# The last 17 slot tiles of the second feed-forward pass in two column halves, and the first chunk's rows in a buffer of their own

## The reference

```
x = x + 0.5 * ffn(layernorm(x))     # 8 experts, top 2, hidden width 352
x = x + attn(layernorm(x))          # 6 heads of 128, causal conv, rotation, scan over tokens
x = x + 0.5 * ffn(layernorm(x))

ffn: scores = x @ gate_w.T + gate_b + bias; the two best experts, gates = softmax of the two
     h = silu(x @ w1[e].T + b1[e]);  y = h @ w2[e].T + b2[e];  out = sum of gate * y over the two
```

## Time and profile before

| | |
|---|---|
| median of three runs | 895.51 us |
| the profiled execution | 895.87 us |
| its span, first to last instruction | 894.1 us |
| TensorE busy | 737.8 us, 83% of the span |
| VectorE busy | 622.1 us, 70% |
| ScalarE, GpSimd busy | 348.1 us and 236.3 us |
| DMA over the span | 137.25 MB, 153 GB/s |

### The profile page before, as it was taken

How to read it: one execution, slowest core, us unless ns; L and a number is a source line. 1 busy time by engine, 2 the same in 40 slices (tenths; PEclk the granted TensorE clock), 3 DMA queues, 4 the chain that set the end, 5 groups by cost and what they waited for, 6 DMA issues and landing times.

```text
span 894.1 us, 13749 instructions
## 1 busy us (share of the span) xinstructions
PE 737.8 (83%) x4128; PEld 406.8 (45%) x4129; DVE 622.1 (70%) x1009; ACT 348.1 (39%) x600; POOL 236.3 (26%) x222
## 2 busy tenths in 40 slices
PE   8527699999990898997999999999529999999910
PEld 5215455555550444443444444444316565656600
DVE  6886755566654269999989998995775555555545
ACT  5714333434320546445644654532703323333300
POOL 3115644444520101101211011021113434444300
PEclk9859999999995899899999999999859999999965
DMA  9936568865425430610441201363836733333269
GB/s 321 385 111 207 186 223 317 322 243 176 143 83 199 99 89 21 121 49 0 88 78 24 60 12 25 120 166 128 311 112 223 255 107 117 117 106 117 84 223 374
DMA packets 45305, 137.25 MB, mean 153 GB/s; under 512 B 5840, under 2 KB 5840, under 8 KB 41936
## 3 DMA queue, kind: packets, MB, share of 16 engines
q1 hardware_dynamic: 27888, 86.38, 26.8%
q0 software_dynamic: 17376, 50.34, 20.5%
HBM read 85.32 MB, written 51.38 MB: 153 GB/s over the span
## 4 chain that ended last, share of the span: by engine, by line
PE 70%; DVE 15%; DMA 5%; issue 4%; ACT 3%; SPq 1%; POOL 0%; DVEq 0%; POOLq 0%; ACTq 0%
PE bank L615 59%; PE bank L609 4%; PE bank L687 3%; DMA space<-y_rows 2%; PE bank L804 2%; DVE space L1469 1%; DVE space L1466 1%; DVE space L1259 1%; DVE bst L1250 1%; SPq L477 1%; DMA y_rows<-space,slot_dst 1%; DVE space L1316 1%; DMA space<-x_in 1%; DMA space<-xn_rows,slot_src 1%; PE bank L738 1%
## 5 line engine op out<-in xcount | busy, mean ns | idle before, releaser
L615 PE MATMUL bank<-space 128*128 (+3 forms) x2958 | 581.0, 349 | 44.5 <-DVE space L1320 25.6
L615 PEld LDWEIGHTS bank<-space 128*128 128x128 f16 (+1 forms) x2958 | 274.3, 99 | 296.2 <-issue 37.7
L541 POOL DMA_INDIRECT y_rows<-space,slot_dst x78 | 99.7, 1278 | 158.2 <-DVE space L1380 158.2
L1361 DVE TENSOR_TENSOR space<-bank,space 128x512 f16<-128x512 f32 x78 | 54.0, 692 | 84.8 <-issue 43.2
L537 POOL DMA_INDIRECT space<-xn_rows,slot_src x78 | 76.3, 978 | 130.4 <-PE bank L609 70.0
L977 ACT ACTIVATE space<-space 128x352 f32<-128x352 f32 x78 | 38.7, 496 | 177.3 <-DVE space L1367 174.8
L1367 DVE SCALAR_TENSOR_TENSOR space<-bank,space 128x352 f32<-128x352 f32 x78 | 40.9, 524 | 64.0 <-PE bank L615 49.1
L609 PE MATMUL bank<-ident,space 128*128 128x128 f32 x440 | 67.6, 284 | 12.4 <-DMA space<-xn_rows,slot_src 10.5
L982 ACT ACTIVATE space<-bank 128x384 f16<-128x384 f32 x78 | 38.3, 491 | 77.9 <-PE bank L687 76.7
L1380 DVE TENSOR_SCALAR space<-bank,slot_gate 128x512 f32<-128x512 f32 x78 | 58.5, 750 | 12.9 <-PE bank L615 10.3
L1466 DVE SCALAR_TENSOR_TENSOR space<-space,cang 128x512 f32<-128x512 f32 x84 | 63.0, 750 | 5.5 <-ACT space L1051 3.3
(11 more groups left out here) (172 smaller groups left out, 697.4 us busy)
## 6 DMA issues: line engine op xcount, KB each, us to landing
space<-ffn_w SPq DMA_DIRECT2D x8, 1472.0 KB, 10.0
w_saved<-space SPq DMA_DIRECT2D x8, 1472.0 KB
space<-w_saved SPq DMA_DIRECT2D x8, 1472.0 KB, 9.5
space<-y_rows SPq DMA_DIRECT2D x40, 256.0 KB, 6.0
xn_rows<-space SPq DMA_DIRECT2D x8, 1024.0 KB, 6.1
space<-x_in SPq DMA_DIRECT2D x7, 1024.0 KB, 5.3
space<-att_w SPq DMA_DIRECT2D x12, 518.0 KB
space<-y_rows POOLq DMA_DIRECT2D x6, 1024.0 KB, 9.3
```

What stands on the lines that cost most here:

```text
L541: gp.indirect_dma_start(y_rows, bass.IndirectOffsetOnAxis(ap=slot_dst[:, t:t + 1], axis=0), yo[:, t % 2], None).then_inc(y_st[t % 2], 16)
L615: last = pe.matmul(dst, a, b, start=(n == 0), stop=(n == len(terms) - 1))
L1361: v.tensor_tensor(xl[:, par], bank[par][:, :], xh[:, par], ALU.subtract).then_inc(m_xl, 1)
```

## The change

**Column halves.** In the second phase, tiles 22 to 38 (`HELD` = 17 tiles) are worked differently. `down` makes only the first 256 of the 512 columns (9 products of 256). The split activations of these 17 tiles are kept (`held_h`, `held_l`). After tile 38, TensorE makes the second 256 columns of all 17 tiles in a second pass. Each half row, 1 KB, is scattered by itself. In the text, pass 1 is tiles 22 to 38 with their first halves, and pass 2 the 17 second halves.

**Loads of the first half.** While pass 2 runs, SyncE loads the first halves of the expert outputs, one DMA of 256 KB (256 rows of 1 KB) for a group of 128 tokens, each released by one more second half that VectorE has taken out of PSUM. From the ninth second half on, VectorE adds a group's first half after each. ScalarE's queue stores the first halves, SyncE's the second halves. The second halves are loaded when all scatters of pass 2 have landed. Their buffers lie on the `w2` weights, those of the first halves on `w1`.

**Order on ScalarE.** In pass 1, `x_high(t+2)` stands ahead of `silu(t+1)`.

**First chunk.** The rows of chunk 0 get a buffer of their own. The wait of SyncE for the last `y_out` is gone, the loads of chunk 0's expert outputs are 4 DMAs in place of 8, chunk 1 is loaded right after them, and the statistics of each 128 rows follow their sum at once. ScalarE has one new wait for the store of chunk 0 (`x1_st`) ahead of the fourth unit.

**Destinations.** The routing makes `slot_dst` in one more VectorE step, and two more small instructions make the destinations of the half rows.

```diff
+LATE = 22
+HELD = SLOT_TILES - LATE
+HALF = D // 2
+AHEAD = 8
...
+        y_halves = y_rows.rearrange("r (h d) -> (r h) d", h=2)
...
-        y_last = Layout(lay.at)([2, NT, D])
+        yo_late = [Layout(moe_at + i * HALF)([HALF]) for i in range(HELD - 1)] + [Layout(lay.at)([HALF])]
...
+        held_h, held_l = (late_h([HELD, KH, P], F16) for _ in range(2))
...
+        y_last = [[Layout(n * half_w - ATT + h * (KD * HID // 2))([2, HALF]) for n in range(NT)] for h in (0, 1)]
...
+        first_at = lay.at
...
+        group_rows = [Layout(first_at)([TPC, D])] + [xgrp] * (NCH - 1)
...
-            sp.wait_ge(m_yo, SLOT_TILES + 2)
...
-                sp.dma_start(xgrp, rows4(x_in, c)).then_inc(cg_in, 16)
+                sp.dma_start(group_rows[c], rows4(x_in, c)).then_inc(cg_in, 16)
...
-                sp.wait_ge(x1_st, 16 * c)
-                sp.wait_ge(c_xn, TPC * c)
+                if c > 1:
+                    sp.wait_ge(x1_st, 16 * c)
+                    sp.wait_ge(c_xn, TPC * c)
                 group_in(c)
...
-                for k in (0, 1):
-                    sp.dma_start(y_first[:, k, i], y_rows[bass.ds(k * T + i * P, P), :]).then_inc(yf_in[i], 16)
+                sp.dma_start(y_first[:, :, i], y_rows[0:2 * T, :].rearrange("(k n p) d -> n p k d", k=2, p=P)[i]).then_inc(yf_in[i], 16)
+            next_group_in(1)
             group_out(0)
-            next_group_in(1)
             group_out(1)
             next_group_in(2)
             group_out(2)
...
+            def halves_in(n, h, done):
+                sp.dma_start(y_last[h][n], y_rows[0:2 * T, h * HALF:(h + 1) * HALF].rearrange("(k n p) d -> n p k d", k=2, p=P)[n]).then_inc(done, 16)
             slots_scattered(1)
-            def outputs_in(n):
-                for k in (0, 1):
-                    sp.dma_start(y_last[:, k, n], y_rows[bass.ds(k * T + n * P, P), :]).then_inc(yl_in[n], 16)
-            def sum_out(n):
+            for n in range(NT):
+                sp.wait_ge(m_yo, 2 * SLOT_TILES + n + 3)
+                halves_in(n, 0, ya_in[n])
+            sp.wait_ge(late_st, 16 * HELD)
+            for n in range(NT):
+                halves_in(n, 1, yb_in[n])
+            for n in range(NT):
                 sp.wait_ge(f_sum, n + 1)
-                sp.dma_start(out[bass.ds(n * P, P), :], rows_last[n // TPC][:, n % TPC]).then_inc(f_out, 16)
...
+                sp.dma_start(out[n * P:(n + 1) * P, HALF:D], rows_last[n // TPC][:, n % TPC, HALF:D]).then_inc(f_out, 16)
+            sp.wait_ge(f_out, 2 * 16 * NT)
...
-                gp.indirect_dma_start(y_rows, bass.IndirectOffsetOnAxis(ap=slot_dst[:, t:t + 1], axis=0),
-                                      yo[:, t % 2], None).then_inc(y_st[t % 2], 16)
+                if ph and t >= LATE:
+                    gp.indirect_dma_start(y_halves, bass.IndirectOffsetOnAxis(ap=half_dst[:, 0, t - LATE:t - LATE + 1], axis=0),
+                                          yo[:, t % 2, 0:HALF], None).then_inc(y_st[t % 2], 16)
+                else:
+                    gp.indirect_dma_start(y_rows, bass.IndirectOffsetOnAxis(ap=slot_dst[:, t:t + 1], axis=0),
+                                          yo[:, t % 2], None).then_inc(y_st[t % 2], 16)
...
+                gp.wait_ge(m_yo, 2 * SLOT_TILES + i + 3)
...
+                                      yo_late[i], None).then_inc(late_st, 16)
             def add_outputs(c, k):
...
+                def down_half(t, i, h, ev):
+                    pe.wait_ge(m_hl, o + LATE + i + 3)
+                    pe.wait_ge(m_yo, o + t + 1)
+                    products(bank[6 + t % 2][:, 0:HALF],
+                             [(a[:, i, c, :], w2(ph, part, c, ev, h)) for c in range(KH)
+                              for a, part in ((held_h, 0), (held_h, 1), (held_l, 0))]).then_inc(m_y, 1)
...
+                def held_steps():
+                    kinds = [expert(LATE)]
+                    for t in range(LATE, SLOT_TILES):
+                        ht(t, t % 2)
+                        if t + 1 < SLOT_TILES:
+                            kinds.append(expert(t + 1))
+                            up(t + 1, 1 - t % 2, kinds[-1])
+                        if t + 2 < SLOT_TILES:
+                            xt(t + 2, t // 2 + 1, t % 2)
+                        down_half(t, t - LATE, 0, kinds[t - LATE])
+                    for i in range(HELD):
+                        down_half(SLOT_TILES + i, i, 1, kinds[i])
...
-                with pe.Fori(PEELED, SLOT_TILES // 2 - 1) as j:
+                with pe.Fori(PEELED, LATE // 2 if ph else SLOT_TILES // 2 - 1) as j:
                     two_steps(j)
...
+                if ph:
+                    held_steps()
+                else:
+                    last_steps()
...
+                def h_high_held(t):
+                    par, i = t % 2, t - LATE
+                    act.wait_ge(m_ht, o + t + 3)
+                    act.activation(held_h[:, i].rearrange("p a b -> p (a b)"), bank[4 + par][:, 0:KH * P], ACT.Copy).then_inc(m_hh, 1)
...
+                if ph:
+                    for t in range(LATE, SLOT_TILES):
+                        h_high_held(t)
+                        if t + 2 < SLOT_TILES:
+                            x_high(t + 2, t % 2)
+                        if t + 1 < SLOT_TILES:
+                            silu(t + 1, 1 - t % 2)
...
+                if u == PAIRS:
+                    act.wait_ge(x1_st, 16)
...
+                act.dma_start(out[n * P:(n + 1) * P, 0:HALF], rows_last[n // TPC][:, n % TPC, 0:HALF]).then_inc(f_out, 16)
...
-                v.tensor_tensor(slot_dst[:, :], second, pad_row, ALU.add)
+                seq(v.tensor_tensor(second, second, pad_row, ALU.add))
+                ch(v.tensor_copy(slot_dst[:, :], second))
+                if ph:
+                    ch(v.tensor_scalar(half_dst[:, 0], second[:, LATE:], 2.0, None, ALU.mult))
+                    ch(v.tensor_scalar(half_dst[:, 1], second[:, LATE:], 2.0, 1.0, ALU.mult, ALU.add))
...
+            def sum_half(n, h, landed_in, done):
+                rows = rows_last[n // TPC][:, n % TPC, h * HALF:(h + 1) * HALF]
+                if h == 0 and n % TPC == 0 and n // TPC < NCH - 1:
+                    v.wait_ge(g_in[n // TPC], landed(n // TPC, 3))
+                v.wait_ge(landed_in[n], 16)
+                seq(v.tensor_tensor(rows, rows, y_last[h][n][:, 0], ALU.add))
+                v.tensor_tensor(rows, rows, y_last[h][n][:, 1], ALU.add).then_inc(done, 1)
...
+                            x_low(t + 2, par)
+                        v.wait_ge(y_st[par], 16 * ((SLOT_TILES // 2 + 1 - par) + t // 2))
+                        y_half(t, i, yo[:, par, 0:HALF])
+                    for i in range(HELD):
+                        y_half(SLOT_TILES + i, i, yo_late[i])
+                        if i >= AHEAD:
+                            sum_half(i - AHEAD, 0, ya_in, a_sum)
...
                     step(2 * j, j, 0)
                     step(2 * j + 1, j, 1)
+                if ph:
...
-                    v.wait_ge(yf_in[i], 32)
-                    seq(v.tensor_tensor(xgrp[:, i], xgrp[:, i], y_first[:, 0, i], ALU.add))
-                    v.tensor_tensor(xgrp[:, i], xgrp[:, i], y_first[:, 1, i], ALU.add).then_inc(c_sum, 1)
+                    v.wait_ge(yf_in[i], 16)
+                    seq(v.tensor_tensor(group_rows[0][:, i], group_rows[0][:, i], y_first[:, 0, i], ALU.add))
+                    v.tensor_tensor(group_rows[0][:, i], group_rows[0][:, i], y_first[:, 1, i], ALU.add).then_inc(c_sum, 1)
                     v.wait_ge(c_sum, i + 1)
+                    ch(v.bn_stats(bst[:, i], group_rows[0][:, i]))
+                ch.wait()
...
-                variance(xgrp)
+                moments()
...
+            for n in range(HELD - AHEAD, NT):
+                sum_half(n, 0, ya_in, a_sum)
             for n in range(NT):
-                rows = rows_last[n // TPC][:, n % TPC]
-                if n % TPC == 0 and n // TPC < NCH - 1:
-                    v.wait_ge(g_in[n // TPC], landed(n // TPC, 3))
-                v.wait_ge(yl_in[n], 32)
-                seq(v.tensor_tensor(rows, rows, y_last[:, 0, n], ALU.add))
-                v.tensor_tensor(rows, rows, y_last[:, 1, n], ALU.add).then_inc(f_sum, 1)
+                sum_half(n, 1, yb_in, f_sum)
 # ---- launch: one core```

TensorE, a step of the loop in the kernel before (tile 2j+1 of `two_steps`): the load of the next expert's number, `ht` (L687), `up` (L615, 352 columns), of which the first products are shown.

```order
L671 TENSOR_LOAD tile_exp
L671 ISA x2
L687 MATMUL bank<-ident,space 128x128 x3
L615 ISA
L615 MATMUL bank<-space 128x352
L615 ISA
L615 MATMUL bank<-space 128x352 x2
```

81 lines of the change are left out of this document (53 added, 28 removed).

## The result

The changed kernel takes 898.71 us (median of 9 runs, 897.63 to 900.79) beside 895.88 for the kernel before: a ratio of 1.0037, 95% interval 1.0027 to 1.0048. It is slower by 0.4% where 1.0% less had been forecast. In two later series on other chips the ratio was 1.0039 and 1.0036. The profiled execution took 898.07, its span is 896.3 us; against the forecast span of 885.0 that is 11.3 us too much.

The account below looks back on a forecast made before the run. Slot tiles were taken as bound by TensorE, the end by DMA. Pass 1 to 842.5, last eviction 863.4, sums to 885.1, span end 889.1, less 4.1 for the first chunk: 885.0, median 886.4 us; range 882.0 to 895.0.

Parts of the forecast that it names:

- the step of 3.95 us: Tiles 22 to 38 with half `down`: 3.95 us from `ht` to `ht`, against 4.67 before.
- the number's read: Load of the expert number between `ht` and `up`: 0.1 us a step, bounds 0 and 0.5.
- the rival of the exposed number load: The load starts only once `ht` has left the sequencer: 0.5 us a step exposed, 892.8 us; chance 0.12.
- Pass 2, 20.9 us: The 17 second halves: nine evictions at 1.0 us, eight at 1.42 with half sums, the last ending at 863.4.
- GpSimd keeps up: Second-half scatters issued beside the evictions at 1.3 us each, the last at about 864.
- The end: After the last eviction: 24 half sums of 0.91 us, 21.7 us, to 885.1, then 4.0 to span end 889.1.
- just hidden: The wait for second-half data, there at 870.3, lies under eight first-half sums on VectorE lasting until 870.7.
- DMA keeps up: At 45 ns for a 1 KB row, DMA ends at 887.7, 1.4 us ahead of VectorE.
- The rival of the dear rows: A 1 KB row costs nearly as much as 2 KB: 901.5 us at 65 ns, 915.5 at 82; chance 0.13.
- The first chunk, 4.1 us: End of the first phase: three groups' statistics end at 283.4, not 287.5; 4.1 us gained, bounds 0.6 and 4.1.
- The clock: Rival: in pass 2 TensorE runs at 1.2 GHz, nine halves take 2.0 us each, 891.4 us; chance 0.03.

Follow-up runs that it names:

- the kernel without scatters: Changed kernel, but the 17 second-half scatters wait until all 17 halves are evicted: 906.35 us, 1.0156 of the kernel before; repeated on another chip, 908.33 us.
- the changed kernel with the number read early: Changed kernel, but TensorE reads the expert number of tile t+2 behind the half product of tile t: 893.85 us, 0.9973 of the kernel before.
- that with 13 tiles: Changed kernel with the expert number read early and the last 13 tiles (26 to 38) in halves, not 17: 893.75 us, 0.9974 of the kernel before.

## Why the prediction was wrong

**Pass 1, the step of 3.95 us.** It measured 4.21 to 4.50, and the term that failed is the number's read: 0.1 had been counted, between bounds of 0 and 0.5, and it is 0.32 at the least and 0.4 on average, which over 15 steps is 4.5 of the 5.3 us. The rest of the step was right, since with the read out of the way it is 3.89 for the 3.85 counted, and in both kernels `ht` waits for `silu`, as forecast. This was the rival of the exposed number load, in mechanism and place; it got a chance of 0.12. The row that spoke for it was taken down to 0.1 with the reason that `ht` hides 0.45 of it. Of that 0.49 it hides 0.17 or less. Against it stood that in the loop such reads cost almost nothing; the trace of before has steps of 4.55 and 4.75 to 4.86 us by turns there, and the longer ones hold the loop's branch and two of its three reads, so it did not show them to be free. The runs give 5.9 us for moving the read, and by itself it turns the sign: without it the kernel is faster than before (0.9973).

**Pass 2, 20.9 us.** It measured 26.6. The terms one by one were right or dear: a half of products 1.0 (0.98), an eviction 484 ns (480), an addition 426 (416 and 426), and the eviction with half sum 1.42, which came out at 1.19, because additions overlap in the records. Without stalls the pass would have been about 19 (the kernel without scatters), 2 us less than forecast. What failed is the pace itself, 1.0 and then 1.42 us for an eviction: it supposed that VectorE hears of a half as soon as it is done. Beside loads and GpSimd's scatters one behind another it heard up to 3.0 us late, and no step of the sum had a term for that. "GpSimd keeps up" was right on its own, at 1.27 for the 1.3 taken. That the last scatter would end the pass, and not the evictions, was seen only as a tie. No rival had the stall; the range to 895 did not reach far enough for it and the read together.

**The end.** The wait that was called "just hidden" was 3.49 us, as the last scatter came at 869.4 and not at 864. The loads followed its issue by 4.8 us (2.73 forecast), and the first sum followed them after 4.25 (3.4). With the half sum at 0.79 and not 0.91, 24 of them take 2.9 us less than counted, a later wait of 0.76 adds to it, and so only +1.8 is left. That the forecast of this part came close is luck: misses of 3 to 4 us against each other.

**DMA keeps up.** Right. In the second halves' sums VectorE waited once for a load, 0.76 us ahead of the third sum, and the 28 additions from there on start 0.34 to 0.45 us apart without a wait, at 350 GB/s and a full share. 16 engines and 1 KB rows give 47 ns a row, forecast 45. The rival of the dear rows, 0.13, is out, though its side of the sign came true. (The fit of 2.0 us + bytes/436 GB/s, which the prediction puts into the section "Measured" of the Trainium skill's page "DMA: Bandwidth & Descriptors", stands there in the section "Anatomy of one DMA — SWDGE (gpsimd) path", for DMAs that GpSimd issues; the loads are SyncE's.)

**The first chunk, 4.1 us.** Right in the mechanism, and in the size by the trace: 4.3 us. The runs of the part alone give less, 2.4 (1.0 to 3.7), so that 4.1 was somewhat too much by them. The last scatter landed after 2.70 us and not 6.3 with the 1 MB load out of its way.

**The clock.** Granted 1.00 through the second pass of this profile, with TensorE busy for 71% of it: the rival did not make this miss. But it exists. In seven of the 13 profiles with a stalled pass, one of them the changed kernel's second, 13 to 29 products ran at 1.2 GHz, 1.4 to 3.0 us more; in the five passes without stalls none did so.

With what was measured, the terms are: before 895.9, first chunk -4.3, the read +6, the stalls +5, which leaves about -4 for the halves by themselves, to 898.7. That last term is a remainder, not a measurement, so the sum closes by construction.

**What stays open.** How scatters 1.27 us apart come to delay the counting of a semaphore between TensorE and VectorE was not seen; the runs show when, not how. Nor do they show whether reads have to run beside the scatters, why tiles with two scatters lose time in the loop and not where they are written out, why one kernel passed smoothly in one profile and stalled in another, or where between 1.27 and 2.0 us the stalls begin. Whether scatters spaced by about 1.5 us would spare both the stalls and the end was not tried.

Three kernels beat both: the first chunk alone (0.9973), the changed kernel with the number read early (0.9973), and that with 13 tiles (0.9974). With the intervals as they are, 0.9958 to 0.9989, none is better than another: splitting the last 17 tiles has, once its read is hidden, gained nothing that can be told from what the first chunk gives.

## What to carry to other kernels

A step that shrinks brings out what it used to hide, and so does a read that moves: between `ht` and `up`, where the step's chain begins, loading one register cost 0.3 to 0.5 us a step, and behind the half `down` nothing that can be seen in the step. Place such reads behind the longest group of products before trusting the new step, and price them by the step with and without them, not by the idle time that the profile shows. Price an added stream of DMA instructions not by its engines' share alone but by its spacing on the issuing engine and by what runs beside it, and ask which of eviction and scatter ends last. And run the unchanged kernel beside the experiments in each series: a cause that seemed plain without it (the array that is read) fell as soon as it ran along.

## What the runs showed of the hardware that was not expected

- Scatters by GpSimd every 1.27 us beside loads make TensorE's finished product known up to 3.0 us late (0.014 otherwise), at a DMA share of 0.52 as at 0.75, with rows of 1 or 2 KB, whichever array is read or written. Without scatters it doesn't happen, nor, but for 0.4 us, with scatters 2.0 to 2.4 us apart, even at a share of 1.08. One profile on one chip passed smoothly all the same.
- SyncE's loads are not needed for it: with two scatters and a gather of GpSimd's in a step, and no other queue moving data, counts came up to 2.2 us late and tiles 8 to 21 took 10.3 us longer, at a share of 0.3.
- Reading one number between two groups of products costs TensorE 0.32 to 0.47 us, of which the trace shows 0.20 as idle in the shortest steps.
- In passes with such stalls the granted clock fell to 0.50 for 13 to 29 products in seven of 13 profiles. The products stood 0.213 us apart and not 0.109.
- Rows of 1 KB take about 47 ns of an engine's time beside 82.5 for 2 KB: 350 GB/s for 397.
- A scatter with a load of 1 MB issued 0.25 us ahead of it let the next loads start after 6.3 us, without it after 2.7.
